# Both mixtures of experts: norm, gate, routing and scatter in five groups of tiles

## The reference, cut to what matters

```python
# L1: scores scale the routed input, no capacity
scores = softmax(x2d @ gate_w.T); top_scores, sel = top_k(scores, 2)
routed_in = x2d[token_idx] * top_scores[:, None]          # sorted by expert
out = scatter_add(swiglu_of_expert(routed_in))            # silu(x w1) * (x w3), then w2
# L2: capacity 1024 per expert, gates scale the output
topv, topi = top_k(xf @ Wr + br, 2); gates = softmax(topv)
rank = cumsum(sel, axis=0) - sel; keep = (sel > 0) & (rank < 1024)
out = scatter_add(gates * (gelu(xg @ W1 + b1) @ W2 + b2)) # only kept pairs
```

## Time and profile before

| | |
|---|---|
| Time, median of 3 runs | 1968.83 us (1964.0 to 1968.96) |
| The profiled execution's own time | 1969.98 us |
| Its span, first to last instruction | 1967.4 us |
| Busy: TensorE, VectorE, ScalarE, GpSimd | 71%, 59%, 36%, 30% of the span |
| Mean granted TensorE clock | 0.799 |

### The profile page before, as it was taken

How to read it: one execution, slowest core, us unless ns; L and a number is a source line. 1 busy time by engine, 2 the same in 40 slices (tenths; PEclk the granted TensorE clock), 3 DMA queues, 4 the chain that set the end, 5 groups by cost and what they waited for, 6 DMA issues and landing times. The chain is left out here.

```text
span 1967.4 us, 43981 instructions
## 1 busy us (share of the span) xinstructions
PE 1397.9 (71%) x14780; PEld 1068.0 (54%) x14780; DVE 1165.4 (59%) x3326; ACT 714.6 (36%) x1769; POOL 590.0 (30%) x1118
## 2 busy tenths in 40 slices
PE   6999889965999730099948999740099646566564
PEld 3777645533777520099936888630088534454453
DVE  4888578877888760044424555460011179969896
ACT  2666456655666400022213455310033212232232
POOL 4555111112110116500047652117500187211231
PEclk9999956777999855599978999955599967677576
DMA  4222100000000001177731110001277511010001
GB/s 147 51 51 51 29 1 2 3 3 18 23 19 22 8 0 45 56 195 206 205 92 44 41 43 24 8 0 47 65 195 201 142 43 35 1 33 11 1 1 43
DMA packets 109071, 108.50 MB, mean 55 GB/s; under 512 B 12656, under 2 KB 88432, under 8 KB 108784
## 3 DMA queue, kind: packets, MB, share of 16 engines
q1 hardware_dynamic: 100720, 89.61, 16.7%
q0 software_dynamic: 8192, 16.79, 3.0%
HBM read 81.19 MB, written 25.17 MB: 54 GB/s over the span
## 5 line engine op out<-in xcount | busy, mean ns | idle before, releaser
L2223 DVE COPY e_xT<-e_pX 128x256 f32<-128x256 f32 x72 | 30.6, 425 | 317.2 <-PE e_pX L2284 317.2
L2284 PE MATMUL e_pX<-W,e_rows 128*128 128x128 f32 x144 | 28.7, 282 | 213.8 <-DMA e_rows<-slots_in 212.6
L2295 PE MATMUL e_H<-e_xT,e_w_up 128*128 128x256 f32 x736 | 174.9, 386 | 1.1 <-DMA e_w_up<-in_f_dram 1.1
L2295 PEld LDWEIGHTS e_H<-e_xT,e_w_up 128*128 128x128 f32 x736 | 136.9, 194 | 18.1 <-DVE e_xT L2223 1.5
L2284 PEld LDWEIGHTS e_pX<-W,e_rows 128*128 128x128 f32 x144 | 18.5, 147 | 216.4 <-DMA e_rows<-slots_in 216.0
L2305 PEld LDWEIGHTS e_pY<-e_w_down,e_h 128*128 128x128 f32 x992 | 119.6, 192 | 23.2 <-issue 16.6
L2305 PE MATMUL e_pY<-e_w_down,e_h 128*128 128x128 f32 x992 | 124.8, 277 | 10.2 <-ACT e_h L2272 9.0
L2144 POOL DMA_INDIRECT slots_in<-R,r_put x96 | 92.0, 959 | 57.1 <-issue 29.0
L428 DVE TENSOR_REDUCE a_mx<-a_S 128x8 f32<-128x1024 f32 x64 | 78.1, 1221 | 34.3 <-PE a_S L513 34.1
L473 ACT ACTIVATE a_PT<-a_ST 128x1024 f32<-128x1024 f32 x64 | 65.5, 1023 | 79.2 <-PE a_ST L540 79.2
L2261 ACT ACTIVATE e_silu<-e_H 128x256 f32<-128x256 f32 x120 | 46.0, 383 | 124.0 <-PE e_H L2295 124.0
(11 more groups left out here) (414 smaller groups left out, 4071.8 us busy)
## 6 DMA issues: line engine op xcount, KB each, us to landing
e_w_up<-in_f_dram SPq DMA_DIRECT2D x40, 384.0 KB, 3.7
e_w_down<-in_f_dram SPq DMA_DIRECT2D x32, 322.0 KB, 3.1
e_rows<-slots_in SPq DMA_DIRECT2D x72, 128.0 KB, 3.0
slots_out<-e_y SPq DMA_DIRECT2D x72, 128.0 KB, 3.6
e_w_up<-in_f_dram SPq DMA_DIRECT2D x32, 256.0 KB, 3.7
e_w_down<-in_f_dram SPq DMA_DIRECT2D x40, 192.0 KB, 3.3
slots_in<-Y SPq DMA_DIRECT2D x32, 160.0 KB, 2.5
a_cK<-in_ctxT_dram SPq DMA_DIRECT2D x64, 64.0 KB, 1.9
```

What stands on the lines that cost most here:

```text
L2295: i = nc.tensor.matmul(H[:, banks * p + b, CHUNK * c:CHUNK * (c + 1)], up[:, p, at:at + P], xT[:, p, :], start=True, stop=True)
```

## The change

- `logits_stage` and `route_stage` become one block, `dispatch_stage`. The tiles go through it in five groups of 4, 4, 8, 8 and 8. For each group the whole chain is done: statistics, norm (straight into R), transposes, gate, choice of the two experts, count, slot numbers, weights, scatter.
- The ranks of a group start at `carry`, the running counts of the groups before. TensorE's count of a group is one "tri" matmul and one "ones" matmul per tile that adds this tile's totals to all later tiles of the group, in place of the scan over tiles. An extra column block gives the group's totals.
- In the first mixture each expert has a region of its own of 4096 slots (`REGION`) in `slots_in`, so a slot number is known when the group is counted. The rows behind a chunk are no longer at chunk times 256: a table `rt.row` is made at the end, and SyncE reads a chunk's row from it before it loads the rows. `slots_out` stays dense, so `rt.get` becomes a table of its own, made at the end too.
- The rows of the first mixture are scaled tile by tile on ScalarE instead of by two large VectorE instructions.
- The transposes and the logits have two PSUM banks each.
- The zeroed area grows to 8 x 4096 rows: 32 pieces of 512 KB from 128 partitions.

`chunk_table` and `output_rows` (not shown) are some 30 small VectorE instructions after the last group, in the first mixture alone.

```diff
+REGION = NTOK
+FILL_P = 128
+FILL_ROWS = E * REGION // (NT * FILL_P)
+GROUPS = ((0, 4), (4, 8), (8, 16), (16, 24), (24, 32))
...
-    slots = net.dram["slots_in"][0:NCH1 * CHUNK, :].rearrange("(n p r) d -> n p (r d)", n=NT, p=FILL_P)
+    slots = net.dram["slots_in"][0:E * REGION, :].rearrange("(n p r) d -> n p (r d)", n=NT, p=FILL_P)
...
+            def take_stats(g):
+                for t in range(*GROUPS[g]):
+                    v.bn_stats(stats[:, t, :], X[:, t, :]).then_inc(s_stats, 1)
+                for t in range(*GROUPS[g]):
+                    dve.wait_ge(s_stats, t + 1)
+                    v.bn_aggr(moments[:, t, :], stats[:, t, :]).then_inc(s_mom, 1)
+            def apply(g):
+                lo, hi = GROUPS[g]
+                dve.wait_ge(s_mom, hi)
+                dve.wait_ge(s_rstd, g + 1)
+                for t in range(lo, hi):
+                    v.tensor_scalar(R[:, t, :], X[:, t, :], moments[:, t, 0:1], rstd[:, 1, t, :],
+                                    ALU.subtract, ALU.mult).then_inc(s_xn, 1)
+            def route(g):
+                lo, hi = GROUPS[g]
+                n = hi - lo
+                wide, ones = [P, n, E], [P, n, 1]
+                Lg = L[:, lo:hi, :]
...
+                dve.wait_ge(s_l, hi // 2)
+                if first:
+                    i = v.tensor_copy(Lg, src)
+                else:
+                    i = v.tensor_tensor(Lg, src, w("f2_br").unsqueeze(1).broadcast_to(wide), ALU.add)
+                i.then_inc(s_ls, 1)
+                dve.wait_ge(s_ls, g + 1)
+                src = Lg
+                for k in range(2):
+                    then(v.tensor_reduce(m[k][:, 0:n, 0], src, AX, ALU.max))
+                    then(v.tensor_tensor(pos[:, 0:n], src, m[k][:, 0:n].broadcast_to(wide), ALU.is_equal))
+                    then(v.tensor_tensor(pos[:, 0:n], pos[:, 0:n], ranks8, ALU.mult))
+                    then(v.tensor_reduce(pm[:, 0:n, 0], pos[:, 0:n], AX, ALU.max))
+                    then(v.tensor_tensor(sel[:, k, 0:n], pos[:, 0:n], pm[:, 0:n].broadcast_to(wide), ALU.is_equal))
+                    if k == 0:
+                        then(v.scalar_tensor_tensor(less[:, 0:n], sel[:, 0, 0:n], -3e38, Lg, ALU.mult, ALU.add))
+                        src = less[:, 0:n]
+                v.tensor_tensor(both[:, 0:n], sel[:, 0, 0:n], sel[:, 1, 0:n], ALU.add).then_inc(s_sel, 1)
+                if first:
+                    then(v.tensor_tensor(ex[:, 0:n], Lg, m[0][:, 0:n].broadcast_to(wide), ALU.subtract))
+                v.tensor_tensor(gap[:, 0:n], m[1][:, 0:n], m[0][:, 0:n], ALU.subtract).then_inc(s_arg, 1)
+                dve.wait_ge(s_cnt, g + 1)
+                base = carry[:, g:g + 1, :]
+                v.tensor_tensor(carry[:, g + 1:g + 2, :], pC[:, n * E:n * E + E].unsqueeze(1), base, ALU.add)
+                v.tensor_tensor(rank[:, 0:n], pC[:, 0:n * E].rearrange("p (n e) -> p n e", e=E),
+                                base.broadcast_to(wide), ALU.add).then_inc(s_rank, 1)
+                dve.wait_ge(s_rank, g + 1)
+                pick = sel[:, :, 0:n]
+                two = [P, TOPK, n, E]
+                if not first:
+                    then(v.tensor_scalar(keep[:, 0:n], rank[:, 0:n], float(CAP), None, ALU.is_lt))
+                    then(v.scalar_tensor_tensor(rank[:, 0:n], w("iota8").unsqueeze(1).broadcast_to(wide), float(CAP),
+                                                rank[:, 0:n], ALU.mult, ALU.add))
+                    for k in range(2):
+                        then(v.tensor_tensor(t3[:, k, 0:n], sel[:, k, 0:n], keep[:, 0:n], ALU.mult))
+                        then(v.tensor_reduce(keptf[:, k, 0:n, 0], t3[:, k, 0:n], AX, ALU.add))
+                for k in range(2):
+                    then(v.tensor_tensor(t3[:, k, 0:n], sel[:, k, 0:n], rank[:, 0:n], ALU.mult))
+                    then(v.tensor_reduce(slotf[:, k, 0:n, 0], t3[:, k, 0:n], AX, ALU.add))
+                sl, kp, du = slotf[:, :, 0:n], keptf[:, :, 0:n], dumpf[:, :, 0:n]
+                if not first:
+                    then(v.tensor_tensor(sl, sl, kp, ALU.mult))
+                    then(v.tensor_copy(rt.get[:, :, lo:hi], sl[:, :, :, 0]))
+                    then(v.tensor_scalar(du, kp, -1.0, 1.0, ALU.mult, ALU.add))
+                    spare = w("spare").rearrange("p (k n) -> p k n", k=TOPK)[:, :, lo:hi].unsqueeze(3)
+                    then(v.tensor_tensor(du, du, spare, ALU.mult))
+                    then(v.tensor_tensor(sl, sl, du, ALU.add))
+                v.tensor_copy(rt.put[:, :, lo:hi], sl[:, :, :, 0]).then_inc(s_idx, 1)
...
+                dve.wait_ge(s_exp, g + 1)
+                if first:
+                    then(v.tensor_reduce(den[:, 0:n, 0], ex[:, 0:n], AX, ALU.add))
+                else:
+                    then(v.tensor_scalar(den[:, 0:n], egap[:, 0:n], 1.0, None, ALU.add))
+                then(v.reciprocal(inv[:, 0:n], den[:, 0:n]))
+                wt = rt.weight[:, :, lo:hi]
+                then(v.tensor_copy(wt[:, 0, :], inv[:, 0:n, 0]))
+                i = v.tensor_tensor(wt[:, 1, :], egap[:, 0:n, 0], inv[:, 0:n, 0], ALU.mult)
+                if not first:
+                    then(i)
+                    i = v.tensor_tensor(wt, wt, kp[:, :, :, 0], ALU.mult)
...
+            take_stats(0)
+            apply(0)
+            for g in range(len(GROUPS)):
+                if g + 1 < len(GROUPS):
+                    take_stats(g + 1)
+                route(g)
+                if g + 1 < len(GROUPS):
+                    apply(g + 1)
+            if first:
+                chunk_table()
+        @block.scalar
+        def _(act):
+            for g, (lo, hi) in enumerate(GROUPS):
+                n = hi - lo
+                for i in range(lo // 2, hi // 2):
+                    act.wait_ge(s_xt, i + 1)
+                    if i >= 2:
+                        act.wait_ge(s_l, i - 1)
+                    nc.scalar.activation(xT[:, i % 2, :], pX[:, i % 2, 0:2 * P], ACT.Copy).then_inc(s_xts, 1)
+                act.wait_ge(s_arg, g + 1)
+                if first:
+                    nc.scalar.activation(ex[:, 0:n], ex[:, 0:n], ACT.Exp)
+                nc.scalar.activation(egap[:, 0:n], gap[:, 0:n], ACT.Exp).then_inc(s_exp, 1)
+                if first:
+                    act.wait_ge(s_wt, g + 1)
+                    act.wait_ge(s_xn, hi)
+                    for t in range(lo, hi):
+                        nc.scalar.activation(Y[:, t, :], R[:, t, :], ACT.Copy,
+                                             scale=rt.weight[:, 0, t:t + 1]).then_inc(s_y, 1)
+                        act.wait_ge(s_y, t + 1)
+                        nc.scalar.activation(R[:, t, :], R[:, t, :], ACT.Copy,
+                                             scale=rt.weight[:, 1, t:t + 1]).then_inc(s_rows, 1)
...
+            for g, (lo, hi) in enumerate(GROUPS):
+                n = hi - lo
+                for i in range(lo // 2, hi // 2):
+                    transpose_x(i)
+                    if i > lo // 2:
+                        gate(g, i - 1)
+                gate(g, hi // 2 - 1)
+                pe.wait_ge(s_sel, g + 1)
+                if g >= 1:
+                    pe.wait_ge(s_rank, g)
+                nc.tensor.matmul(pC[:, 0:(n + 1) * E], w("tri"), both[:, 0:n + 1].rearrange("p n e -> p (n e)"),
+                                 start=True, stop=False)
+                for t in range(n):
+                    k = nc.tensor.matmul(pC[:, E * (t + 1):E * (n + 1)], w("ones"),
+                                         both[:, t:t + 1].broadcast_to([P, n - t, E]),
+                                         start=False, stop=t == n - 1)
+                k.then_inc(s_cnt, 1)
...
+            def take_rstd(g):
+                lo, hi = GROUPS[g]
+                shape = [P, hi - lo, 1]
+                pool.wait_ge(s_mom, hi)
+                nc.gpsimd.tensor_tensor(rstd[:, 0, lo:hi], moments[:, lo:hi, 1:2],
+                                        half[:, 1:2].unsqueeze(1).broadcast_to(shape), ALU.add).then_inc(s_veps, 1)
+                pool.wait_ge(s_veps, g + 1)
+                nc.gpsimd.tensor_tensor(rstd[:, 1, lo:hi], rstd[:, 0, lo:hi],
+                                        half[:, 0:1].unsqueeze(1).broadcast_to(shape), ALU.pow).then_inc(s_rstd, 1)
+            def scatter(g):
+                lo, hi = GROUPS[g]
+                pool.wait_ge(s_idx, g + 1)
+                pool.wait_ge(s_xn, hi)
+                for t in range(lo, hi):
+                    if first:
+                        pool.wait_ge(s_rows, t + 1)
+                    for k in range(TOPK):
+                        rows = Y if first and k == 0 else R
+                        nc.gpsimd.indirect_dma_start(
+                            xg[:, :], bass.IndirectOffsetOnAxis(ap=rt.put[:, k, t:t + 1], axis=0),
+                            rows[:, t, :], None).then_inc(s_put, 16)
+            take_rstd(0)
+            for g in range(len(GROUPS)):
```

(33 more changed lines are left out.)

258 lines of the change are left out of this document (71 added, 187 removed).

## The result

| | before | after |
|---|---|---|
| Median of 4 runs each, side by side | 1966.7 us (1964.0 to 1968.96) | 1939.03 us (1931.33 to 1945.01) |
| Ratio | | 0.985 (0.982 to 0.987) |
| The profiled execution's own time, span | 1969.98, 1967.4 us | 1931.33, 1929.5 us |
| Mean granted TensorE clock | 0.799 | 0.824 |

Faster by 27.7 us, where 44.8 were forecast. The two traces lie further apart than the medians: that of the changed kernel is the quickest of its four runs, and that of before (1969.98 us) is slower than all four of its kernel. Some 7 of the 37.9 us between the two spans lie in stages around the change that run no changed code or gain nothing by it. The stage ahead of the first mixture's attention took 181.8 us instead of 187.3, at a granted clock of 0.72 against 0.66. So I compare stages, not whole spans.

The account below looks back on a forecast made before the run. Dispatch was taken as bound by norm and gate, a VectorE chain and 80.8 us of GpSimd scatters in series. 1969.98 - 59.5 (dispatch) + 14 (experts) + 0.7 (first read) = 1925.2, median 1924 us; range 1890 to 1950.

Parts of the forecast that it names:

- count of 8 tiles, 4.7 us: Dispatch, steady groups of 8 tiles: TensorE's count matmuls, which VectorE waits for, were priced at 4.7 us per group.
- the loop's 23.4: First mixture's dispatch: period per 8-tile group, closed by ScalarE, 23.4 us against GpSimd's 20.2, starving it 3.2 us.
- The tail: End of each dispatch: 7.4 us from the last scatter's end to the experts' first read of rows.
- The experts: First mixture's experts: SyncE's row read makes it the bound, 14 us more; first read 0.7 us; lower bound 0.
- the room of 0.38 us: First mixture's experts: SyncE's wait for TensorE per chunk, taken as room to absorb part of the 0.65 us read.
- No slowdown of the scatters: Dispatch: GpSimd's scatters were to keep their 1.263 us pace although VectorE now works beside them.
- The 1930 that this rule gave: Whole kernel if VectorE's norms and copies lock GpSimd out, some 3 us per group: about 6 us more, 1930.
- The fill: First attention: zeroing 32 x 512 KB, each landing in 3.7 us within a 6.2 us iteration; nothing, at most 5 us.
- (a): Rival, dispatch: GpSimd is never starved, 98 us saved instead of 59.5, hence 1886 us; chance 0.14.
- (b): Rival, first experts: SyncE's read costs 1.3 us per chunk, 35 us instead of 14, hence 1945; chance 0.15.
- (c): Rival, first attention: 512 KB fills take 8.0 us each, context loads queue, 67 us more, 1991 us; chance 0.03.
- (d): Rival, dispatch: scatter issue does not overlap the groups' steps, 183 us per mixture, 2041 us in all; chance 0.03.

Follow-up runs that it names:

- e1: Changed kernel without the row-table read: first mixture's rows loaded from chunk times 256, so experts compute on other rows; 1917.79 us, ratio 0.977.
- e5: Changed kernel with the first mixture's row-table read and row load on ScalarE's queue instead of SyncE's; 1915.97 us, ratio 0.972.
- e8: Changed kernel with the edits of e5, e6 and e7 together; 1884.31 us, ratio 0.957.
- e4: Changed kernel with all 64 scatters of a mixture issued only after the last group's indices; 2021.46 us.
- e7: Changed kernel with norms one group ahead, power steps in the middle of scatter runs, next group's copies ahead of and between the scalings; 1903.16 us, ratio 0.966.
- e6: Changed kernel with the count's matmul operands in bfloat16, sums still float32; 1922.2 us, median of three executions, ratio 0.975.

## Why the prediction was right in direction and its gain too high

**The groups' loop: the term "count of 8 tiles, 4.7 us" failed.** Without scatters in flight it was even too high (4.04 and 4.05). In groups 3 and 4, beside them, it took 8.07 to 10.87 us. I had priced a TensorE step by its own records and by nothing that happens between its end and the engine behind it. The period from group 3's carry to group 4's in the first mixture, taken apart (row times of the changed kernel; forecasts from the loop's 23.4):

| | forecast | measured |
|---|---|---|
| indices, weights | 2.5 | 2.3 (734.71 to 737.04) |
| 16 scalings | 7.2 | 5.9 (to 742.97) |
| gate and VectorE up to the count | 9.0 | 9.1 (to 752.11) |
| count until the carry | 4.7 | 9.35 (to 761.46) |
| sum | 23.4 | 26.75 |

The third row contains 1.2 us by which the logits came late, so its other steps were cheaper than forecast by about as much.

The lateness was 10.8 us in the first mixture and 10.9 in the second. The rest of the chain was cheaper than forecast: group 2's scatters started 47.1 and 50.1 us after the stage's start, 3.9 us ahead of the forecast in both (51.0 and 54.0), and the shorter scalings and counts gave 4 us more in groups 3 and 4 of the first mixture. 97.8 - 3.9 + 10.8 - 4.0 = 100.7, and the last group's scatters started at 100.6. In the second mixture they started at 100.2, not 96.4. The same terms there are 96.4 - 3.9 + 10.9, less 1.3 for the two counts' own matmuls and 1.7 for the other steps of group 4's period (22.91 us from carry to carry, of which 14.8 are not the count, where 16.5 were forecast): 100.4.

**The tail.** From the last scatter's end to the first read 9.1 and 8.1 us, not 7.4: 1.7 and 0.7 us. In the first mixture 1.0 us of it is the first read of the row table, since e1, without it, has 8.1; the forecast had this read, at 0.7 us, among the experts. No run shows why the rest is longer. Both dispatch stages so end 4.3 us above the forecast, 8.6 us together.

**The experts.** +17.9 us against 14.7 forecast. The mechanism (SyncE full, TensorE waits) was right: the stage is back at 172 us when the read goes (e1) or moves to another queue with its load (e5). The read's price was right too, 0.69 us where I took 0.65. The term that was mis-sized is what is left per chunk: 0.55 us between SyncE's issues (4.72 - 4.13 = 0.59 by the stretches shown), where 0.65 - 0.38 = 0.27 was the plain sum and 14 us stood for 0.37. Of the room of 0.38 us, an average of waits over 160 us, 0.22 was filled, and SyncE's other steps grew by 0.08. So 0.69 - 0.22 + 0.08 = 0.55 us, over some 33 chunks 18 us.

**What held.** Power step for 8 columns: 1.67 us (I took 1.5). VectorE's pace: 0.26 us. No slowdown of the scatters: 0.962 us each at the median, while VectorE was busy 6.59 us of the 22 us of group 2's run. The Trainium skill (SBUF — State Buffer, "Who interferes with whom") would have had the eight norms lock GpSimd out. The trace does not agree. In the first mixture nearly all of them are over before the run starts, but in the second they run beside it:

```profile
1303.09 1.03 POOL L2177 DMA_INDIRECT slots_in<-R,r_put  x1 [8.48 <-DVE r_put L2024]
...
1303.65 2.13 DVE L1965 TENSOR_SCALAR R<-X,d_moments,d_rstd 128x128 f32<-128x128 f32 x8
1304.43 0.96 POOL L2177 DMA_INDIRECT slots_in<-R,r_put  x1 [0.30 <-issue]
...
1305.69 0.96 POOL L2177 DMA_INDIRECT slots_in<-R,r_put  x1 [0.30 <-issue]
```

The two scatters beside 2.13 us of norms took 0.96 us each and started 1.26 us apart, as with VectorE at rest (1.263). The trace does not tell in which mode the norms ran. The 1930 that this rule gave lies nearer the result, but for another reason. The fill: 512 KB landed in 3.2 us (I took 3.7), and the attention was no longer than before.

**The rivals.** (a), GpSimd never starved, falls for this kernel: the four gaps of the first mixture come to 24.2 us. But e8 reached the time it named, 1884 against 1886, by another road, since it gained more in the experts and less in the groups. (b), SyncE's read at 1.3 us, falls: it costs 0.69 us, and the stage 17.5 us, not 35. (c), the fill, falls. (d), no overlap, falls: e4 is what it would have looked like, 174 us per mixture.

**The sum.** Forecast 44.8 us. Dispatch came 8.6 short, the experts 3.2, and two stages that were to stay equal another 2.6 (second experts 0.5; the attention between the mixtures, 261.8 us before and 263.9 after, 2.1), together 14.4. That leaves 30.4, against 27.7 between medians. The last 2.7 us lie within the spread of the runs (13.7 us).

## What to carry to other kernels

When a step is moved under GpSimd's scatters, do not price the chain by its instructions alone. Here hand-overs of the count cost 4 to 7 us more, those of the logits 0.5 to 2, and early ones nothing. Put work that does not need the result into the wait: e7 took back 16 and 14 us so. A queue whose waits add up to 0.38 us per step had 0.22 us of room. Put an added read on a queue that is idle (e5) before you count it as a price of the idea.

## What the runs showed of the hardware

- While GpSimd issued indirect scatters, the report of TensorE's last count matmul of groups 3 and 4 came 4.0 to 8.2 us after the modelled end in float32 (8.97 and 11.6 us in e7's group 4) and 2.5 to 6.6 us in bfloat16 (e6; 6.8 and 0.5 us in e8's group 4). In float32 it came 0.03 to 0.05 us after it with no scatter in flight, beside plain transfers at 141 GB/s, and also in group 1 of the changed kernel, beside the sixth to eighth scatters. Two engines that waited for it started within 0.01 us of each other. The size did not depend on the bytes per row (64 or 512).
- Other reports were late beside scatters too: the gate's to VectorE by 0.5 to 2.0 us in the changed kernel and up to 4.2 us in e6, and in e7 VectorE started 1.9 us after its own result before, with nothing else to wait for.
- GpSimd's power step grew with the columns: 0.70 us for 2, 1.02 for 4, 1.67 for 8.
- The third register read added 0.69 us between two of SyncE's issues, of which its load row shows 0.27 us.
